# Attention layer on one core: O's halves added before the turn, two heads per turn, a transfer issued by ScalarE, a loop body of two batches

## What is computed

```
h = jnp.maximum(_layernorm(x, axis=-1), 0.0)
q = (h @ Wq + bq).reshape(b, n, H, HD)      # k and v alike
scores = jnp.einsum('bihd,bjhd->bhij', q, k) / jnp.sqrt(jnp.float32(HD))
scores = scores + mask[None, None, :, :]
weights = jax.nn.softmax(scores, axis=-1)
out = jnp.einsum('bhij,bjhd->bihd', weights, v)
x = x + out.reshape(b, n, H * HD)
```

## Time and profile before

| what | value |
|---|---|
| time, median of 3 runs | 4150.72 us (4150.56 to 4152.28) |
| the profiled execution's own time | 4145.39 us |
| its span from first to last instruction | 4143.3 us |
| granted TensorE clock over the span | 0.999 |
| busy: PE, PEld, DVE, ACT, POOL | 98%, 81%, 75%, 76%, 32% |

### The profile page before, as it was taken

How to read it: one execution, slowest core, us unless ns; L and a number is a source line. 1 busy time by engine, 2 the same in 40 slices (tenths; PEclk the granted TensorE clock), 3 DMA queues, 4 the chain that set the end, 5 groups by cost and what they waited for, 6 DMA issues and landing times.

```text
span 4143.3 us, 77847 instructions
## 1 busy us (share of the span) xinstructions
PE 4075.5 (98%) x22528; PEld 3339.6 (81%) x22528; DVE 3111.1 (75%) x5128; ACT 3142.6 (76%) x5642; POOL 1313.3 (32%) x1665
## 2 busy tenths in 40 slices
PE   7999999999999999999999999999999999999999
PEld 6888888888888888888888888888888888888887
DVE  6877868778677786777767677786877768767687
ACT  5877868778687786877868688686886868868687
POOL 4333332333323333333333233332333333333222
PEclk9999999999999999999999999999999999999999
DMA  5221212212122221222212122121221212212111
GB/s 178 72 75 57 82 46 78 67 57 82 57 68 67 60 85 60 59 68 75 69 60 68 59 77 67 60 77 49 77 67 60 80 47 77 73 54 85 47 52 31
DMA packets 219597, 282.56 MB, mean 68 GB/s; under 512 B 12304, under 2 KB 143376, under 8 KB 210576
## 3 DMA queue, kind: packets, MB, share of 16 engines
q1 hardware_dynamic: 219152, 277.14, 22.2%
HBM read 172.23 MB, written 37.75 MB: 51 GB/s over the span
## 4 chain that ended last, share of the span: by engine, by line
PE 92%; ACT 2%; issue 2%; DMA 2%; POOL 1%; DVE 1%; SPq 0%; POOLq 0%; ACTq 0%; DVEq 0%
PE T L528 20%; PE misc L486 17%; PE S L516 11%; PE S L517 11%; PE O L540 10%; PE O L547 10%; PE misc L499 8%; PE misc L555 3%; DMA xln<-in_x 2%; PE misc L465 1%; ACT yparts L636 1%; ACT probs L653 1%; ACT pT L645 0%; DVE pT L811 0%; DVE bn L769 0%
## 5 line engine op out<-in xcount | busy, mean ns | idle before, releaser
L811 DVE TENSOR_TENSOR pT<-T,pT 128x512 fp32r<-128x512 f32 x2048 | 1401.5, 687 | 758.4 <-ACT pT L645 745.7
L645 ACT CAST pT<-T 128x512 fp32r<-128x512 f32 x2048 | 1189.0, 592 | 654.2 <-PE T L528 553.4
L805 DVE CUSTOM_DVE_ANT_0 S<-S,mask 128x1024 f32<-128x1024 f32 x1024 | 1257.4, 1228 | 10.0 <-issue 4.9
L528 PEld LDWEIGHTS T<-ident,probs 128*128 128x128 f32 x8192 | 1012.5, 140 | 270.1 <-ACT probs L653 14.1
L528 PE MATMUL T<-ident,probs 128*128 128x128 f32 x8192 | 1226.3, 272 | 3.7 <-DVE pT L811 2.9
L653 ACT ACTIVATE probs<-S,negmax 128x1024 f32<-128x1024 f32 x1024 | 1151.1, 1124 | 8.9 <-DVE negmax L805 5.8
L547 PE MATMUL O<-pT,vs 128*64 128x512 f32 x2048 | 975.6, 476 | 0.2 <-DVE pT L811 0.2
L540 PE MATMUL O<-pT,vs 128*128 128x512 f32 x2048 | 817.5, 399 | 14.0 <-issue 13.9
L486 PE MATMUL misc<-hT,wqk 128*128 128x512 f32 x3036 | 788.4, 395 | 8.1 <-ACT yparts L636 7.7
L486 PEld LDWEIGHTS misc<-hT,wqk 128*128 128x128 f32 x3036 | 557.0, 188 | 158.8 <-issue 25.7
L403 POOL TENSOR_TENSOR yparts<-yparts 128x256 f32<-128x256 f32 x256 | 188.3, 736 | 1112.4 <-ACT yparts L636 1112.4
(11 more groups left out here) (70 smaller groups left out, 3703.3 us busy)
## 6 DMA issues: line engine op xcount, KB each, us to landing
wqk<-wqk_split SPq DMA_DIRECT2D x63, 1024.0 KB, 7.0
xln<-in_x SPq DMA_DIRECT2D x240, 256.0 KB, 4.2
xres<-in_x SPq DMA_DIRECT2D x66, 512.0 KB, 3.7
kA<-kA SPq DMA_DIRECT2D x128, 256.0 KB, 3.2
kB<-kB SPq DMA_DIRECT2D x128, 256.0 KB, 3.8
out<-xres SPq DMA_DIRECT2D x64, 512.0 KB, 3.2
probs<-in_adj SPq DMA_DIRECT2D x4, 1024.0 KB, 4.9
wqk_split<-vs SPq DMA_DIRECT2D x3, 1024.0 KB, 10.5
```

The costliest lines, as they stand in the source:

```text
L528: mm = pe.transpose(T[:, u % 2, i * P:(i + 1) * P], probs[:, (GB * g + i) % RING, j * P:(j + 1) * P], ident[:])
L645: act.copy(pT[:, u % PT, 0, :], T[:, u % 2, :]).then_inc(p_hi, 1)
L805: dve.tensor_tensor_reduce(S[:, s % 2, :], S[:, s % 2, :], mask[:, s % NB, :], 1.0, 3.0e38, ALU.add, ALU.min, negmax[:, s % RING:s % RING ...
L811: dve.tensor_tensor(pT[:, u % PT, 1, :], T[:, u % 2, :], pT[:, u % PT, 0, :].bitcast(F32), ALU.subtract).then_inc(p_lo, 1)
```

## The change

Each group's O is still copied to `oT`, but is not turned on its own. ScalarE, after the copy and one `probs_hi`, issues a transfer inside SBUF (`move_o`) that takes one half of `oT`'s rows to the partitions where the head's result belongs in a new buffer `oP`; GpSimd adds the other half there (`sum_o`, slot 5 of the next group). So `oP` holds, for one half of the query rows, the summed O of two heads in its 128 partitions. When the second head is in, TensorE turns both at once: `turn_out` stands at slots 2 and 10 of the next pair only (OUT_AT), not at slots 2, 10, 18 and 26. GpSimd's `finish` then scales and adds 512 columns in two operations, at slots 3 and 17 of a pair (FINISH_AT).

`xres` loses its second buffer and shares the tensor `outs` with `oP`. SP's queue is written per slot: the store at slot 19 of a pair, the reload at 24, k's copies at 8 and 15. The statistics of the next batch stand at eight slots in pairs 0 and 1, the transpositions of its x tiles at 77, 79, 83, 85, 88, 91, 94, 96 instead of 83, 85, 87, 88, 91, 92, 95, 96. `invert` (DVE) moves from slot 2 to slot 4 of a group. The loop runs 7 times over a body of two batches.

```diff
-HT_SLOTS = (83, 85, 87, 88, 91, 92, 95, 96)
+HT_SLOTS = (77, 79, 83, 85, 88, 91, 94, 96)
...
-STATS_SLOTS = ((5, 7, 13), (37, 39, 45), (69, 71))
+STATS_SLOTS = (5, 7, 11, 13, 37, 39, 43, 45)
...
+COPY_K_AT, STORE_AT, RES_AT, WQK_AT = (8, 15), 19, 24, (21, 21, 28, 21)
+
+OUT_AT, FINISH_AT = (2, 10), (3, 17)
+PER = UNITS // PAIRS
...
+            def sum_o(b, g, last=False):
+
+                n, half, second = GROUPS * b + g, g % 2, (g // 2) % 2
+                rows = slice(HD * second, HD * second + HD)
...
+                gp.wait_ge(o_moved, 16 * (n + 1))
+                gp.tensor_tensor(oP[rows, half, :], oP[rows, half, :], oT[rows, :], ALU.add).then_inc(o_summed, 1)
...
+            def finish(b, p, half):
+
+                n = 2 * (PAIRS * b + p) + half
                 gp.wait_ge(y_copied, n + 1)
...
+                gp.wait_ge(inverted, GROUPS * b + 4 * p + 2 + half + 1)
+                gp.tensor_tensor(y[:], y[:], rinv[:, half].unsqueeze(3).to_broadcast([P, GB, 2, HD]),
                                  ALU.mult).then_inc(y_scaled, 1)
...
-            def turn_out(b, g, free):
-                pe.wait_ge(o_copied, GROUPS * b + g + 1)
+            def turn_out(b, p, half, free):
+
+                pe.wait_ge(o_summed, GROUPS * b + 4 * p + 2 + half + 1)
                 pe.wait_ge(*free)
                 for i in range(GB):
-                    mm = pe.transpose(misc[:, i * P:(i + 1) * P], oT[:, i * P:(i + 1) * P], ident[:])
+                    mm = pe.transpose(misc[:, i * P:(i + 1) * P], oP[:, half, i * P:(i + 1) * P], ident[:])
                 mm.then_inc(o_turned, 1)
...
+            def move_o(b, g):
+
+                n, half, second = GROUPS * b + g, g % 2, (g // 2) % 2
+                act.wait_ge(o_copied, n + 1)
+                used = 2 * (PAIRS * b + g // 4) + half - 1
+                if some(used):
+                    act.wait_ge(o_turned, used)
+                own, other = (slice(0, HD), slice(HD, P))[::-1 if second else 1]
+                act.dma_start(oP[own, half, :], oT[other, :]).then_inc(o_moved, 16)
...
                     probs_hi(b, u)
+                    if u == 1 and not first:
+                        move_o(b - 1, GROUPS - 1)
+                    if u > 1 and u % NB == 1:
+                        move_o(b, u // NB - 1)
...
-            with act.Fori(1, B - 1) as b:
-                body(b)
+            with act.Fori(0, B // 2 - 1) as two:
+                body(2 * two + 1)
+                body(2 * two + 2)
```

More of the change, by code:

```diff
@@ L280, in _ @@
                 load_xln(1, t)
-            for p in range(2):
-                load_xres(0, p)
+            load_xres(0, 0)
             sp.wait_ge(qk_mm, 4)
@@ L288, in body @@
             def body(b, first=False, last=False):
[L289 to L301, removed]
+                for u in range(UNITS):
+                    p, v = u // 32, u % 32
+                    if u == 0 and not first and not last:
+                        sp.wait_ge(h_turned, NB * (b + 1))
+                        for t in range(XLN):
+                            load_xln(b + 1, t)
+                    if v == STORE_AT and not (first and p == 0):
+                        sp.wait_ge(y_added, 2 * (PAIRS * b + p))
                         if p == 0:
@@ L305, in body @@
                             store(b, p - 1)
[L306 to L324, removed]
-                    if not (last and p == PAIRS - 1):
-                        copy_k(b, p + 1, 1)
@@ L327, in body @@
-                    if not (last and p >= PAIRS - 2):
+                    if v == RES_AT and not (first and p == 0):
+                        sp.wait_ge(stored, 16 * (PAIRS * b + p))
+                        load_xres(b, p)
+                    if u in STATS_AT and not last:
+                        t = STATS_AT[u]
+                        sp.wait_ge(bn_done, NB * (b + 1) + t + 1)
+                        load_xln(b + 1, (t + XLN) % NB)
+                    for half in range(2):
+                        if v == COPY_K_AT[half] and not (last and p == PAIRS - 1):
+                            copy_k(b, p + 1, half)
@@ L416, in _ @@
+                dst = xres[:, GB * half:GB * half + GB, :]
+                gp.tensor_tensor(dst, dst, y[:].rearrange("p i l d -> p i (l d)"), ALU.add).then_inc(y_added, 1)
             for t in range(0, NB, 2):
@@ L433, in body @@
                 for u in range(UNITS):
+                    if u % NB == LAG + 3 and not (first and u == LAG + 3):
+                        if u == LAG + 3:
+                            sum_o(b - 1, GROUPS - 1)
+                        else:
+                            sum_o(b, u // NB - 1, last)
                     if u in STATS_AT and not last:
@@ L618, in _ @@
                 contract_lo(B - 1, u)
-            turn_out(B - 1, GROUPS - 1, (y_copied, GROUPS * B - 1))
+            for half in range(2):
+                turn_out(B - 1, PAIRS - 1, half, (y_copied, 2 * (PAIRS * B - 1) + half))
         @block.scalar
```

142 lines of the change are left out of this document (77 added, 65 removed).

## The result

The changed kernel takes **4111.73 us** (4110.51 to 4114.69, four runs) beside 4150.64 us (4150.38 to 4152.28, four runs) of the kernel before: ratio 0.9906, 95% interval 0.9889 to 0.9924, or 38.9 us saved. The profiled execution took 4110.51 us against 4145.39, 34.9 us less. The forecast was 4098 us with a range from 4070 to 4134: the sign and the main mechanism (turns of O taken off TensorE) hold, the point is 13.7 us too low, and one term, the loop's, came out with the wrong sign.

What follows compares the result with a forecast made beforehand. TensorE was taken to set the pace, VectorE and ScalarE close behind. Terms -56.3 + 11.5 + 9.6 - 18 - 7.5 + 2 + 6 gave -52.7 us: 4092.7 profiled, 4098 us as median, range 4070 to 4134.

Steps and rivals of the forecast that it cites:

- Turns, -56.3: TensorE: half of the 256 turns of O go, 128 at 0.44 us each, -56.3 us.
- the rival in which it doesn't: VectorE at 92% in the bare stretch: time freed on TensorE is waited away, 4143 us; chance 0.08.
- Chain at a group's start, +11.5: Slots 17 and 25, turn gone: ScalarE-VectorE chain leaves TensorE 0.09 us short at 128 places, +11.5 us.
- ScalarE's issue, +9.6: ScalarE issues 256 transfers of 0.4 us; the delay is paid in full at slots 35, 67, 99, +9.6 us.
- d: How late the issue makes a group's second cast, taken as 0.2 us; free in 128 turnless places up to 0.41.
- (c): Slots 1 and 9 of a pair: nearby fills of 1.4 us and more cover the second cast's delay.
- New path's latency, 0: Transfer (3.2 us for twice the bytes) and GpSimd's add (1.30 us) finish before O's next copy or turn; cost 0.
- x tiles, -18: Slots 77 to 95: fills no longer wait behind a turn's copy, fewer tiles late; net -18 us, bounds -25 and 0.
- a queue is late: Single `xres`, k's copies ahead of a tile, or pair 3's weights cost 1 to 2 us per batch; chance 0.08.
- Loop, -7.5: Loop's turn: 13 waits of 13.9 us become 6 turns, -7.5 us.
- Statistics, +2: Slot 11: statistics of about 0.9 us nearly hidden in VectorE's 1.00 us idle, +2 us.
- tail, +6: End of run: an added transfer of about 2.5 us and longer GpSimd operations before the store, +6 us.

Runs made afterwards that it cites:

- experiment 7: Changed kernel with four unused transpositions of a constant put back at slots 18 and 26 of each pair, where turns of O had been: 4150.13 us, ratio 0.999.
- experiment 6: Changed kernel with ScalarE's transfer cut into two of 256 columns, 512 issues in all: 4288.51 us, ratio 1.0331.
- experiment 4: Changed kernel with ScalarE's transfer issued at slot 2 of a group, behind the copy out of `misc`, instead of slot 1: 4098.43 us, ratio 0.9878.
- experiment 5: Changed kernel with the transfer between the halves issued by SP instead of ScalarE: 4094.86 us, ratio 0.9863.
- Experiment 3: Changed kernel with k's second copy at slot 16 of a pair instead of 15, behind the load of x tile 3: 4098.07 us, ratio 0.9878.
- experiment 10: Changed kernel, two-batch body, with 41 transpositions of a constant at TensorE's start to move its loop's code: 4094.98 us, ratio 0.9875.
- experiment 11: Kernel before with 350 long-fulfilled waits (175 instructions) at TensorE's start, moving its loop to place 162: 4163.77 us, ratio 1.0028.
- Experiment 2: Kernel before with only its loop changed to a body of two batches: 4133.45 us, ratio 0.9963.
- experiment 9: Changed kernel with a one-batch loop body and 41 transpositions of a constant at TensorE's start, loop at place 243: 4102.33 us, ratio 0.9886.
- experiment 1: Changed kernel with its loop put back to a body of one batch on every engine: 4111.53 us, ratio 0.9908.
- experiment 8: Changed kernel with one-batch body, k's second copy at slot 16, and ScalarE's issue behind the copy out of `misc`: 4091.61 us, ratio 0.9854.
- experiment 12: Changed kernel with 41 transpositions at TensorE's start, k's second copy at slot 16, and ScalarE's issue behind the `misc` copy: 4064.86 us, ratio 0.9797.

## Why the prediction was right, and where it was wrong

**Turns, -56.3.** Right, in size and in kind: experiment 7 puts turns and chain together at 44 to 49 us (56.3 - 7.3 = 49.0), and the bare stretch came out at 21.96 against 22.1. TensorE does set the pace, which leaves nothing of the rival in which it doesn't, although VectorE is at 93% of the stretch. The reading of headroom in the Trainium skill, *Perfetto Trace Analysis*, weighed in the prediction, would have put us at 4143 us (the page names the share of the peak rate, MFU, beside weight loads, and that was not worked out); weight loads went from 81% to 80%, and the time fell all the same.

**Chain at a group's start, +11.5.** The mechanism is right (138 waits for VectorE's low part, gone in experiment 7). The term was 0.09 us a place and measured 0.06, 7.3 us.

**ScalarE's issue, +9.6.** +10.1, from two errors that cancel: the issue takes 0.47 us, not 0.4, so d is 0.29 instead of 0.2; and of d only 0.21 reaches TensorE, where the forecast had "every bit". That it costs nothing in the 128 places up to d = 0.41 is in line. (c), the cover at slots 1 and 9, holds at this d only: in experiment 6, with d more than three times as large, slots 10 and 11 were the dearest place. The issue is small beside the transfer (0.47 against 3.1 us), as the Trainium skill, *DMA: Bandwidth & Descriptors*, section "Issuing engines are not separate DMA queues", has it. But it was ScalarE's time, and taking it off the path (experiments 4 and 5) brought 13 us.

**New path's latency, 0.** Right: transfer 3.1 us, add 1.29 us, and starting it a slot later (experiment 4) loses nothing.

**x tiles, -18.** This term failed in size: -5.5. The part on the copy behind a turn came true (slot 83 fell from 0.36 to 0.06 us, slot 87's late tile from 0.75 to nothing). But the forecast had named tile 3, queued on SP behind k's copies, and left 5 us for it; it takes 0.86 us in each batch, 12.8 us in all. Experiment 3 gave 13.7 us back with one number. The rival "a queue is late" had thus the right place, and the forecast the wrong price for it.

**Loop, -7.5.** This is the step that failed: "13 waits of 13.9 us; 6 turns are left". The turns cost 7.8 us more, not 7.5 less, 15.3 us off and the largest part of the error (13.7 us by the medians, 17.8 by the profiled executions; the x tiles' 12.5 too much and slot 16's 5.7 too little come next). The forecast took the price of a turn as fixed. It isn't: it changes with where the loop's code lies. Experiments 10 and 11 show it from both sides, with the work in the loop untouched: 81 instructions ahead of the loop take 17 us off the changed kernel, 175 put 12.6 us on the kernel before. Experiment 2 clears the body's length. What was true in the step is that six turns are cheaper than thirteen at the same place (8.1 against 17.7 us).

That the second stop depends on the loop's place in a block of 256 is shown for the one-batch loop (place 243 in the kernel before and experiment 9: no stop; place 162 in experiments 1 and 11: a stop). For the 2.5 us stop of the two-batch loop the packets show what goes with it: two blocks fetched at almost the same time instead of one, in each of the 34 dear turns and in none of the 85 others. Which instructions each packet carries the trace doesn't say, so that one of the two is not needed is an argument. The place of the loop's start doesn't fix this stop: at place 162 the one-batch loop (experiments 1, 8 and 11) has one packet and the short stop, and in experiment 7, whose start and end both moved (64 instructions and a longer body), the same turn was dear four times and cheap twice. What decides between the two stays open.

**Statistics, +2; tail, +6.** No loss shows in slots 11 to 13, and the tail cost +5.9.

**Not forecast.** Slot 16 lost 0.43 us in each batch before and 0.07 now (-5.7). It fell to 0.25 with the loop's form alone (experiment 2), so part of it is no effect of O's path; and with the turns put back (experiment 7) it stays low, so the rest is no effect of the missing turns. What it is wasn't tested. Slots 22 and 54 lose 0.13 us more each. That is gone or nearly so (0 to 0.7 us in all) in the four experiments with TensorE's code of the changed kernel moved (7, 9, 10 and 12), so it seems to belong to the code's place as well. Its cause, and the 4 us in no row, stay open.

## What to carry to other kernels

When an engine's instructions lie in a loop whose body is some thousands long, the turn has no fixed price, neither from one version to the next nor always from one turn to the next: read the idle time at the turn and in the first slots behind it in every version, and if it has moved without a cause in the work, try to shift the loop by some instructions before judging the edit itself; here the place alone was worth 12 to 17 us, of 39 for the whole change. An issue of a transfer costs its engine real time, so put it beside a long instruction of that engine rather than between two that others wait for. And where a load shares a queue with copies that wait, ask what stands ahead of it: one slot earlier or later was 13 us.

## What the hardware showed that I had not expected

- A turn of TensorE's loop lost 1.35 us (two-batch body, place 243), 2.4 us (one-batch, place 162, in two stops) or 4.2 us (two-batch, place 162). The last stands 2.3 to 2.7 us still; three of six such turns then have some 3.4 us at the lower clock, the other three stay at 1.00 and stop again in slot 0. At the turns with stops of 0.7 to 1.5 us the clock stayed at 1.00.
- The long stops are those with two packets of instructions on TensorE's queue at almost the same time (34 of 34 turns), the short ones those with one (85 of 85).
- TensorE's instructions come in packets of 16 KB, 209 of them in 4.1 ms, on a queue of their own; at 0.4% of the transfer time they are invisible in the busy shares, yet move the time by 17 us.
- A transfer's issue on ScalarE took 0.47 us nearly without spread (0.468 to 0.522). It began during the cast ahead of it, so an issue doesn't wait for an empty engine, but the instruction behind it does wait for the issue. A second one directly behind took 0.62 us in more than half of the cases and up to 2.1 us in the others, and not because SP issued at the same time.
- GpSimd's add of 64 x 512 took 1290 ns, the one of 128 x 512 1287 ns: half the partitions is no time saved.
